# Attention of an audio tower in rounds of one head pair and both batches

## The reference, cut to what matters

```
h  = gelu(x[:, 1:] @ W1 + x[:, :1] @ W2 + b)          # token mixing, row 0 is the readout
z  = layernorm(h)
q, k, v = z @ Wq.T, z @ Wk.T, z @ Wv.T                 # 16 heads of 64, inner size 1024
h += softmax(q k^T / 8) v @ Wo.T + bo                  # per batch and head, 255 keys
z2 = layernorm(h)
h += sum over the 2 best of 8 experts: p_e * (silu(z2 @ w1[e]) @ w2[e])
   + sigmoid(z2 @ gate_w) * ((silu(gate) * up) @ down) # shared expert
```

## Time and profile before

| | |
|---|---|
| median of 3 runs | 1110.76 us (1110.05 to 1113.36) |
| the profiled execution | 1112.86 us |
| its span, first to last instruction | 1111.1 us |
| PE busy | 1051.8 us (95%) |
| PEld (weight loads) busy | 880.7 us (79%) |
| DVE busy | 757.1 us (68%) |
| ACT busy | 673.6 us (61%) |
| POOL busy | 512.6 us (46%) |
| mean granted TensorE clock | 0.987 of full speed |

### The profile page before, as it was taken

How to read it: one execution, slowest core, us unless ns; L and a number is a source line. 1 busy time by engine, 2 the same in 40 slices (tenths; PEclk the granted TensorE clock), 3 DMA queues, 4 the chain that set the end, 5 groups by cost and what they waited for, 6 DMA issues and landing times.

```text
span 1111.1 us, 23557 instructions
## 1 busy us (share of the span) xinstructions
PE 1051.8 (95%) x8042; PEld 880.7 (79%) x8042; DVE 757.1 (68%) x1975; ACT 673.6 (61%) x2067; POOL 512.6 (46%) x557
## 2 busy tenths in 40 slices
PE   6979999999999999999999999999997979999996
PEld 5867778878787887887788778878775869998985
DVE  3756775786778577667857766775775656666667
ACT  4647774775677477567747756774775545554531
POOL 0024543546446364645546464554435376444430
PEclk9989999999999999999999999999999989999999
DMA  8110000001000000100000010000003733444369
GB/s 265 59 44 1 1 1 20 2 1 40 19 1 23 19 20 1 40 20 1 21 21 21 1 40 20 1 11 30 21 1 105 252 101 103 134 133 133 123 215 309
DMA packets 47498, 65.93 MB, mean 59 GB/s; under 512 B 7992, under 2 KB 39480, under 8 KB 47384
## 3 DMA queue, kind: packets, MB, share of 16 engines
q1 hardware_dynamic: 40056, 44.50, 12.8%
q0 software_dynamic: 7056, 19.93, 5.3%
q10 hardware_dynamic: 272, 0.00, 0.0%
HBM read 36.09 MB, written 28.33 MB: 58 GB/s over the span
## 4 chain that ended last, share of the span: by engine, by line
PE 70%; POOL 7%; DVE 6%; issue 6%; DMA 3%; ACT 2%; SPq 1%; another core or an unknown queue 0%; DVEq 0%; POOLq 0%; ACTq 0%
PE pT_ps L714 10%; PE o_ps L727 9%; PE proj_ps L69 9%; PE proj_ps L71 9%; PE proj_ps L70 8%; PE s_ps L700 8%; POOL prob L1655 2%; PE v_ps L69 2%; PE v_ps L70 2%; PE v_ps L71 2%; POOL prob L1657 2%; PE s_ps L69 2%; DMA back<-expert_out_rows 2%; PE s_ps L70 2%; PE s_ps L71 2%
## 5 line engine op out<-in xcount | busy, mean ns | idle before, releaser
L1015 ACT ACTIVATE prob<-s_ps,nmax 128x255 f32<-128x255 f32 x512 | 238.7, 477 | 228.1 <-DVE nmax L1222 228.0
L1655 POOL TENSOR_SCALAR prob<-prob,rinv 128x255 f32<-128x255 f32 x128 | 139.4, 1089 | 375.0 <-DVE rinv L1240 370.6
L1222 DVE TENSOR_REDUCE nmax<-s_ps 128x2 f32<-128x510 f32 x256 | 166.3, 682 | 37.8 <-PE s_ps L700 36.3
L714 PEld LDWEIGHTS pT_ps<-ident,prob 128*128 128x128 f32 x1024 | 109.6, 141 | 60.7 <-issue 49.8
L714 PE MATMUL pT_ps<-ident,prob 128*128 128x128 f32 x1024 | 146.0, 281 | 6.7 <-POOL prob L1657 3.5
L1247 DVE COPY probT<-pT_ps 128x512 f32<-128x512 f32 x128 | 88.5, 691 | 76.9 <-PE pT_ps L714 76.9
L727 PE MATMUL o_ps<-probT,v 128*64 128x256 f32 x1024 | 139.6, 394 | 1.2 <-DVE oT_lo L1253 1.2
L700 PE MATMUL s_ps<-qk_space 64*128 64x256 f32 x1536 | 125.4, 296 | 5.3 <-ACT prob L1015 4.6
L1657 POOL TENSOR_SCALAR prob<-prob,rinv 128x255 f32<-128x255 f32 x128 | 118.9, 929 | 0.0
L700 PEld LDWEIGHTS s_ps<-qk_space 64*128 64x128 f32 x1536 | 99.2, 185 | 21.9 <-issue 8.7
L1015 ACT ACTIVATION_READ_ACCUMULATOR prob<-s_ps,nmax 128x1 f32 x512 | 106.5, 208 | 0.0
(11 more groups left out here) (265 smaller groups left out, 2717.8 us busy)
## 6 DMA issues: line engine op xcount, KB each, us to landing
xg<-expert_in_rows SPq DMA_DIRECT2D x71, 130.0 KB
back<-expert_out_rows SPq DMA_DIRECT2D x6, 1024.0 KB, 21.2
xin<-in_x_dram SPq DMA_DIRECT2D x8, 512.0 KB, 4.6
z_rows<-z SPq DMA_DIRECT2D x8, 512.0 KB, 3.2
z<-z_rows SPq DMA_DIRECT2D x8, 512.0 KB, 5.8
expert_in_rows<-bo_row SPq DMA_DIRECT2D x16, 128.0 KB
raw_up<-in_L_ffn_w_dram SPq DMA_DIRECT2D x8, 256.0 KB, 4.8
raw_down<-in_L_ffn_w_dram SPq DMA_DIRECT2D x8, 256.0 KB, 6.2
```

The lines of the kernel that those rows point to most:

```text
L714: m = pe.transpose(pT_ps[h][:, o:o + P], prob[u_par(i)][:, h, qt, kt * P:(kt + 1) * P], ident[:])
L1015: m = act.activation(prob[u_par(i)][:, h, qt, 1:N], s_ps[h][:, qt * N + 1:(qt + 1) * N], ACT.Exp, bias=nmax[u_par(i)][:, n:n + 1], accum_o ...
L1222: dve.tensor_reduce(nmax[u_par(i)][:, 2 * h:2 * h + 2], s_ps[h][:].rearrange("p (q k) -> p q k", q=2)[:, :, 1:N], AX_X, ALU.max, negate=Tr ...
L1655: pool.tensor_scalar(prob[k][:, 0, 1, 1:N], prob[k][:, 0, 1, 1:N], rinv[k][:, 1:2], None, ALU.mult).then_inc(s_nA1, 1)
```

## The change

A round is one head pair with both batches of the group, w = 8 g + p. There are 64 rounds (`LAST`), and a projection is made two rounds ahead (`AHEAD`).

- TensorE does in round w: the values of w - 1 of both batches, the scores of w + 1 of both batches, the transposes of (w, batch 0), Q of w + 2, the transposes of (w, batch 1), K of w + 2, then the group's step of output or routing (`between`), then both V tiles of w + 2.
- Banks: four for scores (`s_ps[b][h]`), two for transposes, `o_ps` for values and K, and one `proj_ps` for Q and V. The output rows and the router use the scores' banks of batch 1. z's transposes use the transposes' banks.
- The values of both batches lie in one bank and are copied in one 512-column step (`o_hi`, `o_lo`), and so are two tiles of V (`v_copy`). Probabilities and inverse sums are held for four units.
- The order on ScalarE, VectorE and GpSimd follows the rounds. The router's steps lie in rounds 0 to 7 of the next group.
- The last round interleaves the output products with the last values.
- z2's transposed parts lie in the end of `oT_hi` and `oT_lo`, so SP waits for the last logits before it loads experts 4 to 7; h's second buffer lies in `prob2` and `prob3`.

The diff, cut to its core:

```diff
@@ banks and buffers
-        prob = [sb(f"prob{i}", [P, 2, 2, N]) for i in range(2)]
+        prob = [sb(f"prob{i}", [P, 2, 2, N]) for i in range(4)]
-        s_ps = [bank(f"s_ps{h}") for h in range(2)]
+        s_ps = [[bank(f"s_ps{b}{h}") for h in range(2)] for b in range(2)]
-        proj_ps = [bank(f"proj_ps{j}") for j in range(2)]
-        v_ps = bank("v_ps")
+        proj_ps = bank("proj_ps")
+        qk_ps = (proj_ps, o_ps)
-        z_ps, gate_ps, up_ps, rows_ps = (v_ps, o_ps), s_ps, pT_ps, proj_ps
+        z_ps, gate_ps, up_ps, rows_ps = (proj_ps, o_ps), s_ps[0], pT_ps, s_ps[1]
@@ sync
             load_z3(3)
+            sp.wait_ge(s_lg, GROUPS)
             for e in range(RAW_FIRST, E):
@@ tensor
+            def project_qk(w, n):
+                if n == 0:
+                    if w:
+                        pe.wait_ge(s_ve, w)
+                elif w < AHEAD + 1:
...
+                else:
+                    pe.wait_ge(s_ol, w - AHEAD)
...
+            def project_v(w):
+                p = w % PAIRS
+                pe.wait_ge(s_qkl, 2 * w + 1)
+                for j in (2 * p, 2 * p + 1):
...
+            def scores(w, b):
+                pe.wait_ge(s_qkl, 2 * w + 2)
+                if w:
+                    pe.wait_ge(s_exp, 2 * (u - 2) + 2)
...
+            def transpose_p(w, b):
...
+                    pe.wait_ge(free, u + FREE_B)
...
+            def values(w):
+                pe.wait_ge(s_ve, PAIRS * (w // PAIRS) + 2 * (p // 2) + 2)
+                pe.wait_ge(s_qkl, min(2 * (w + AHEAD) + 2, 2 * LAST))
...
+            def between(g, r):
+                q, R = g - 1, PAIRS * g + r
+                exps_done = min(2 * (2 * (R + 1) + 1) + 1, 4 * LAST)
+                if r == 0:
+                    pe.wait_ge(s_ol, PAIRS * g)
+                    for j in range(2):
+                        pe.wait_ge(s_exp, exps_done + j)
+                        output_rows(q, j)
+                elif r == 2:
+                    pe.wait_ge(s_z2, GT * q + GT)
+                    for c in range(DC):
+                        pe.wait_ge(s_exp, exps_done + c)
+                        transpose_z2(q, c)
+                elif r == 3:
+                    pe.wait_ge(s_exp, exps_done)
+                    router_logits(q)
+                elif r == 5:
+                    pe.wait_ge(s_exp, exps_done)
+                    router_ranks(q, rows_ps[0])
...
+            def round_of(g, r):
+                w = PAIRS * g + r
+                if w:
+                    values(w - 1)
+                scores(w + 1, 0)
+                if g and r:
+                    between_read(g, r - 1)
+                scores(w + 1, 1)
+                transpose_p(w, 0)
+                if w + AHEAD < LAST:
+                    project_qk(w + AHEAD, 0)
+                transpose_p(w, 1)
+                if w + AHEAD < LAST:
+                    project_qk(w + AHEAD, 1)
+                if g:
+                    between(g, r)
+                if w + AHEAD < LAST:
+                    project_v(w + AHEAD)
+                if r == LAST_OLD and g + 1 < GROUPS:
+                    for c in range(DC):
+                        transpose_z(g + 1, c)
...
@@ scalar
+            def round_of(g, r):
+                w = PAIRS * g + r
+                if w:
+                    o_hi(w - 1)
+                exps(w + 1, 0, 0)
+                exps(w + 1, 0, 1)
+                probT_a(w, 0)
+                exps(w + 1, 1, 0)
+                exps(w + 1, 1, 1)
+                if w + AHEAD < LAST:
+                    qk_hi(w + AHEAD, 0)
+                normalise_b1(w + 1, 0)
+                if g and r == 4:
+                    router_exps(g - 1)
+                probT_a(w, 1)
+                if w + AHEAD < LAST:
+                    qk_hi(w + AHEAD, 1)
+                normalise_b1(w + 1, 1)
+                if g and r == 2:
+                    for c in range(DC):
+                        z2_hi(g - 1, c)
+                if w + AHEAD < LAST:
+                    v_copy(w + AHEAD)
...
@@ vector
+            def round_of(g, r):
+                w, q = PAIRS * g + r, g - 1
+                maxima(w + 1, 0, 0)
+                maxima(w + 1, 0, 1)
+                if w:
+                    o_lo(w - 1)
+                maxima(w + 1, 1, 0)
+                maxima(w + 1, 1, 1)
+                if g and r == 1:
+                    row_stats(q, 0)
+                    row_stats(q, 1)
+                probT_b(w, 0)
+                normalise_a(w + 1, 0)
+                if g and r == 4:
+                    probabilities(q)
+                elif g and r == 6:
+                    places(q)
+                normalise_a(w + 1, 1)
+                if w + AHEAD < LAST:
+                    qk_lo(w + AHEAD, 0)
+                probT_b(w, 1)
+                if g and r == 4:
+                    best_two(q)
+                if w + AHEAD < LAST:
+                    qk_lo(w + AHEAD, 1)
...
@@ gpsimd
+            def round_of(g, r):
+                if w + 1 < LAST:
+                    normalise_b(w + 1, 0)
+                if g and r == PAIRS - 1:
+                    scatter_rows(q, 1)
+                if w + 1 < LAST:
+                    normalise_b(w + 1, 1)
...
```

More of the change, by code:

```diff
@@ L673, in project_qk @@
                 for c in range(DC):
[L674 removed]
+                    if p == 0 and n == 0:
                         pe.wait_ge(s_zl, DC * g + c + 1)
[L676 removed]
+                    m = three(pe, qk_ps[n][:], hi[:, c, cols], lo[:, c, cols], zT_hi[:, c, :], zT_lo[:, c, :],
                               c == 0, c == DC - 1)
                 m.then_inc(s_qk, 1)
[L680 to L685, removed]
[L686 removed]
@@ L713, in transpose_p @@
                             o = kt * N + qt * P
-                            m = pe.transpose(pT_ps[h][:, o:o + P], prob[u_par(i)][:, h, qt, kt * P:(kt + 1) * P], ident[:])
+                            m = pe.transpose(pT_ps[h][:, o:o + P], prob[u % 4][:, h, qt, kt * P:(kt + 1) * P], ident[:])
                     m.then_inc(s_T, 1)
[L717 to L728, removed]
+            def values(w):
+                p = w % PAIRS
+                pe.wait_ge(s_ve, PAIRS * (w // PAIRS) + 2 * (p // 2) + 2)
+                pe.wait_ge(s_qkl, min(2 * (w + AHEAD) + 2, 2 * LAST))
+                if w:
+                    pe.wait_ge(s_ol, w)
+                pe.wait_ge(s_pA, 2 * w + 2 + FREE_B)
+                pe.wait_ge(s_pB, 2 * w + 2 + FREE_B)
+                vt = v[(p // 2) % 2]
+                for b in range(2):
+                    for kt in range(2):
+                        for h in range(2):
+                            col = (p % 2) * P + h * DH
+                            m = pe.matmul(o_ps[h * DH:(h + 1) * DH, b * N:(b + 1) * N], vt[:, 2 * b + kt, col:col + DH],
+                                          probT[b][:, h, kt, :], start=kt == 0, stop=kt == 1)
@@ L1136, in _ @@
             hidden_split_hi(0, 0)
-            router_step(GROUPS, 3)
-            router_step(GROUPS, 4)
+            for c in range(DC):
+                z2_hi(GROUPS - 1, c)
             z3_hi(1)
@@ L1481, in _ @@
                 z_lo(0, c)
-            for j in range(4):
-                qk_lo(0, j)
-                if j == 1:
-                    maxima(0, 0, 0)
-                    maxima(0, 0, 1)
-                    normalise_a(0, 0)
+            qk_lo(0, 0)
+            qk_lo(0, 1)
+            for b in range(2):
+                for h in range(2):
+                    maxima(0, b, h)
+            qk_lo(1, 0)
+            normalise_a(0, 0)
+            qk_lo(1, 1)
+            normalise_a(0, 1)
             dve.wait_ge(s_r, 1)
@@ L1684, in group, with router_rstd @@
-            def group(g, first, last):
-                for i in range(UNITS):
-                    if i + 1 < UNITS:
-                        normalise_b(g, i + 1)
-                    elif not last:
-                        normalise_b(g + 1, 0)
-                    if not first:
-                        router_step(g, i)
-                    if i == 0 and not last:
-                        layernorm_rstd(g + 1)
-                    if 3 <= i < 3 + GT and not last:
-                        layernorm_apply(g + 1, i - 3)
-                    if 9 <= i < 9 + GT and not last:
-                        add_bias(g + 1, i - 9)
+            def router_rstd(q):
+                pool.wait_ge(s_mv2, GT * q + GT)
+                pool.tensor_scalar(var_eps2[:], mean_var2[:, :, 1], EPS_LN, None, ALU.add).then_inc(s_var2, 1)
+                pool.wait_ge(s_var2, q + 1)
+                pool.tensor_tensor(rstd2[:], var_eps2[:], half_neg[:], ALU.pow).then_inc(s_rstd2, 1)
```

678 lines of the change are left out of this document (319 added, 359 removed).

## The result

The changed kernel takes **1163.3 us** (1158.5 to 1169.5) against 1111.2 (1110.1 to 1113.4) of the kernel before on the same chip: ratio 1.0469, interval 1.0444 to 1.0495. The forecast was 1147 with a range of 1118 to 1172. The sign and the mechanism were as forecast; the size was 16 us too small. The profiled execution took 1162.59, its span is 1160.9.

What follows compares the result with a forecast made beforehand. TensorE set the pace before; regrouping would save it 33 us, but a rigid chain would bind. Stage +31.7, omitted steps +4, tail -2, clock +3 gave +36.7: 1149.5 profiled, 1147 us median, 8-in-10 range 1118 to 1172.

Steps and rivals of the forecast that it cites:

- The chain: Plain round, scores to scores: maxima, eight exponentials, `normalise_a`, Q's low part, V, then values in fixed order, 10.88 us.
- TensorE's stand: Plain round: TensorE stands 0.9 us before V, with short stands before the second transposes 1.3 us idle in all.
- r0: Round 0 of a group: 96 output products take 11.5 us, 21.5 in all, an extra of 10.6.
- r1: Round 1: four row statistics (1.76 us) ahead of `probT_b` on VectorE, about 0.8 of it spare; +1.0.
- r3: Round 3: the logits' 32 products (1.78 us) fit TensorE's stand for 0.9; +0.9.
- r2: Round 2: z2's transposes fit TensorE's stand, so no extra time.
- r4: Round 4: `probabilities` ahead of the second `normalise_a` waits for router exponentials, ending at 8.3 us instead of 6.1; +2.2.
- r6: Round 6: taken as plain; `places` left out, with `best_two` 0 to 1 us a group, 4 us added in all.
- The clock: TensorE's long stand in r4 brings seven slow-clock stretches of up to 1.7 us, 0 to 12 in all, 3 taken.
- A: Rival: TensorE's work binds, rounds of 9.56, faster at 1078 us, or about 1085 with r4; chance 0.12.
- B: Rival: chain and work about cancel, a round of 10.3, 1111 us; chance 0.03.
- C: Rival: loop as forecast, but idle time brings the slow clock in one of two rounds, 53 us more, 1200; chance 0.07.

Runs made afterwards that it cites:

- experiment 3: The change as made plus one VectorE copy of 128x512 ahead of Q's low part in every round: 1189.4 us, ratio 1.070, plain round 11.52.
- experiment 4: The change as made plus the same VectorE copy of 128x512, but behind K's low part: 1167.6 us, ratio 1.0519, plain round 10.99.
- experiment 7: experiment 6 with VectorE's `probT_b(w, 0)` ahead of batch 1's maxima: 1102.7 us, ratio 0.9967, plain round 10.47.
- experiment 9: experiment 7 with ScalarE's `probT_a` copies earlier and `router_rstd` ahead of GpSimd's normalisations: 1080.3 us, ratio 0.9704, plain round 10.15.
- experiment 2: The change as made with VectorE's routing steps behind K's low part and row statistics in round 0: 1124.9 us, ratio 1.0119.
- experiment 1: The change as made with Q's copies earlier on ScalarE and VectorE: 1159.1 us, ratio 1.0419, plain round 10.77.
- experiment 12: experiment 9 with K's low part ahead of the second `normalise_a` on VectorE: 1064.1 us, ratio 0.9632, plain round 9.75.
- experiment 5: experiment 1 plus K's high part ahead of `normalise_b1` and `probT_b(w, 1)` ahead of the second `normalise_a`: 1156.9 us, ratio 1.0446.
- experiment 6: experiment 5 with the router's work ordered as in experiment 2: 1105.1 us, ratio 0.9991, plain round 10.50.
- experiment 8: experiment 7 with the first transposes between the two batches' scores, two more changes of product kind a round: 1107.8 us, ratio 1.0028.
- experiment 10: The kernel before, with V's products between scores and values in twelve of sixteen units: 1180.1 us, ratio 1.0612.

## Why the prediction was right, and where it was off

**The chain (right).** Forecast 10.88 for a plain round, measured 11.01, every link but one within 0.03; the wait named is V's for `qk_lo`. Experiments 3 and 4 show it by cause: in a plain round, time ahead of that step costs 0.95 of itself, behind it nothing. The off term is V, 1.63 for 1.50: the first product behind a stand takes 0.38 instead of 0.28, and the next starts 0.22 later instead of 0.12. I had taken V from a unit in which TensorE never stood. Over 62 rounds this 0.13 less small gains is +7 us.

**TensorE's stand (right).** With 0.23 from one 512-column product to the next, V could have followed Q and K at 377.92 and began at 378.73, a stand of 0.81; the second transposes could have begun at 375.18 and began at 375.60 (released by ScalarE's `probT`), a stand of 0.42. Together 1.23, forecast 0.9 and 0.4. The forecast put the second down to both copies; experiments 7 and 9 show that only ScalarE's binds in a plain round; VectorE's binds in round 1, behind the row statistics.

**Routing rounds.** Extras over a plain round, forecast and measured: r0 10.6 and 10.6; r1 1.0 and 0.9; r3 0.9 and 0.9; r5 0.9 and 0.9. The forecast's group is 102.8 by its own terms (87.2 and 15.6; it has 102.9), measured 105.5. Three terms failed:
- "r2: z2's transposes fit the stand" looked at TensorE alone. The step that cost is `z2_rows` on VectorE, moved next to a step that waits for GpSimd: +0.5 in the groups without slow clock, +2 us.
- r4, +2.2 forecast, +3.2 measured. The delay of V was right to 0.1, but `best_two` delays K's low part, and the second way to the values, which had 0.2 to spare in a plain round, then has none.
- r6, 0 forecast, +0.5 measured. `places` stands ahead of the second `normalise_a`, in the first chain itself: V begins 8.00 us into round 6 of group 2 and 7.50 into round 7.

I had seen `best_two` and `places` and taken 4 us for them in the stage; they cost 10. In all, the forecast had 29 us for router steps in the chain's way (7 × 3.2 for r1 and r4, these 4, and 3 for the clock); experiment 2, which moves them, is 38 us faster than the change as made.

**The clock.** Seven stretches forecast in r4 at up to 1.7, of which I took 3 us; there were four in the routing rounds, three of them in r1. They cost about 5 before what round 2 gives back. Same order of size, another place.

**The first rounds.** The first scores to the second 7.25 (8), round 0 of group 0 13.88 (10.9 + 3). Against the forecast stage of 803 (796 + 4 + 3): plain +7, r2 +2, r4 and r6 +6, clock +2, the rest -2, together the 15 that were missing. The tail is +1, the start -1 and what follows -2, which makes the 13 between 1149.5 and 1162.59, the forecast and the measured profiled execution.

**Rivals.** A (TensorE binds, 1078 to 1085) was wrong for this kernel, since it needs the chain to be shorter than 9.56, and right about what is behind it. But what it named as enough, Q's copy early, was not: in experiment 1 V no longer waits, and the round is 10.77. With the whole order mended (experiment 12) the round is 9.75 and the ratio 0.963, which on the 1110.76 shown is 1070. B (cancelling, a round of 10.3) is excluded by 11.01. C (31 slow stretches) is excluded by the four among the routing rounds. But its mechanism was underestimated: in experiments 1 and 5 shorter plain rounds with the router's work in its old place met 11 and 12 stretches.

**My own misses in the experiments.** Five expectations of time (experiments 1, 5, 6, 7, 9) were too low. In 1, 5, 6 and 9 I removed the last wait, and the next wait stood closer behind it than I had counted; in experiment 7 the copy that I moved was not the one waited for; in experiments 1 and 5 the slow clock came on top. Experiments 8 (14 us less than expected) and 10 (53 us more) missed as prices of a change. Why the slow clock came in groups 1, 4 and 7 and not in the others after the same stand stays open.

## What to carry to other kernels

When a kernel merges two units to save switches on its busiest engine, write down the chain from one block to the next through the other engines, in the order of their streams, with every buffer that is shared anew: it binds before their busy shares say so, and it is mended by moving copies, not by removing work. Do that for the second-latest way as well; each step of mending here moved a plain round by only 0.03 to 0.4 us, to the next wait, until TensorE was busy in 98.4% of the stage. Occasional work belongs behind the last step that a bank waits for, and steps that wait for another engine need their producer moved up too.

## What the runs showed of the hardware

- A change between products of 64 rows and whole-array products costs TensorE 0.18 us (2.83 against 2.47 for two), without any wait shown. The price is for scores and transposes in turn.
- The first 128x256 product after a stand takes 0.38 us instead of 0.28, and the next begins 0.22 later instead of 0.12. A stand isn't the only case: behind the router's 32-column products, without a wait, it took 0.37 (experiment 9, 326.08).
- A stand of 1.55 us in round 1, 0.25 in the same round aside, was followed by a stretch at a granted clock of 0.50 (the 1.2 GHz level) in three groups of seven and by none in the other four; it cost 1.5 us there, of which the next round gave 0.5 back. What decides between them is not shown. Where the router's steps caused no stand (experiments 2, 6, 9 and 12), the clock stayed full through all the groups with routing.
